# Down products with the activations held in TensorE, a rebuilt opening and new due times, in a transformer layer with 32 routed experts

## The reference, cut to what matters

```python
x = x + attn(layernorm(x), W_attn, W_proj)
x = x + ffn(layernorm(x), ...)

# attn: 16 heads of 8 channels; q against sums of k over blocks of 4, 8, ... 1024
# tokens and against the tail of the own block of 4; softmax; the same sums of v;
# out @ W_proj.T
# ffn: 32 experts of 64 hidden channels, 6 chosen for each token, 1 shared of 256
h = relu2(einsum('th,eih->tei', x, up_w)) * combine[:, :, None]
moe_out = einsum('tei,ehi->th', h, down_w)
shared = relu2(x @ shared_up_w.T) @ shared_down_w.T
return moe_out + shared
```

## Time and the profile before

| what | value |
|---|---|
| median of 3 runs | 650.69 us (650.59 to 652.74) |
| profiled execution, its own time | 650.5 us |
| its span, first to last instruction | 648.4 us |
| mean granted clock of PE | 0.930 of full speed |
| busy share of PE, DVE, ACT, POOL | 86%, 59%, 59%, 44% |

### The profile page before, as it was taken

The page is one execution under the profiler, slowest core; times in us unless marked ns, Lnnn a source line. Parts: engine busy times, 40 slices in busy tenths (PEclk is TensorE's granted clock), DMA queues, the critical chain, the costliest instruction groups (busy, mean ns, idle before and its releaser), DMA issues.

```text
span 648.4 us, 10506 instructions
## 1 busy us (share of the span) xinstructions
PE 560.4 (86%) x3568; PEld 271.1 (42%) x3568; DVE 380.3 (59%) x935; ACT 380.4 (59%) x543; POOL 282.1 (44%) x403
## 2 busy tenths in 40 slices
PE   1434778888897999889999979999998999999997
PEld 1132123243343435345445334544445434566553
DVE  2626876966878583677756991765767703605400
ACT  1310136674654686467675568677666698675764
POOL 2400303702622573335535662436436424565675
PEclk9755579898997998979999989999999999999999
DMA  6484000184320208605214049334205222234352
GB/s 154 132 210 86 1 3 3 45 208 129 83 68 25 79 4 226 178 35 129 75 50 136 31 126 211 104 85 105 75 27 162 71 67 82 85 114 144 102 175 87
DMA packets 49337, 63.45 MB, mean 98 GB/s; under 512 B 8484, under 2 KB 30788, under 8 KB 48004
## 3 DMA queue, kind: packets, MB, share of 16 engines
q1 hardware_dynamic: 49284, 62.78, 35.7%
HBM read 50.31 MB, written 12.06 MB: 96 GB/s over the span
## 4 chain that ended last, share of the span: by engine, by line
PE 58%; DVE 17%; SPq 9%; DMA 6%; issue 4%; ACT 3%; POOL 2%; POOLq 0%; DVEq 0%; ACTq 0%
PE sums_ps L1060 16%; PE ring L1048 13%; PE sums_ps L992 9%; DVE MXR L1162 6%; SPq L598 6%; PE ring L975 4%; PE ring L953 3%; DMA XP<-in_x_dram 3%; PE ring L913 2%; PE ring L970 2%; PE ring L999 2%; PE ring L1027 2%; PE ring L947 2%; DMA WB<-combine 2%; DMA QA<-MB 1%
## 5 line engine op out<-in xcount | busy, mean ns | idle before, releaser
L727 POOL TENSOR_TENSOR H<-RV,WB 128x512 f32<-128x512 f32 x128 | 164.2, 1295 | 164.5 <-ACT RV L830 130.1
L819 ACT ACTIVATE PT<-ring 128x1024 f32<-128x1024 f32 x160 | 158.5, 1022 | 96.5 <-PE ring L975 95.8
L1162 DVE TENSOR_REDUCE MXR<-ring 128x4 f32<-128x1024 f32 (+2 forms) x192 | 176.0, 952 | 61.3 <-PE ring L953 58.3
L1060 PE MATMUL sums_ps<-H,wdown 128*128 128x512 f32 x288 | 149.4, 616 | 1.4 <-POOL H L727 1.1
L877 ACT ACTIVATE RV<-ring 128x512 f32<-128x512 f32 x144 | 85.5, 594 | 74.8 <-PE ring L1048 72.8
L992 PE MATMUL sums_ps<-PT,VA 128*32 128x512 f32 (+1 forms) x768 | 91.7, 560 | 0.0
L1048 PE MATMUL ring<-XH,WUH 128*128 128x512 f32 x144 | 80.8, 561 | 2.4 <-DVE MB L1273 1.7
L830 ACT ACTIVATE RV<-RV 128x512 f32<-128x512 f32 x128 | 80.6, 630 | 3.7
L975 PE MATMUL ring<-QA,KA 54*128 54x512 bf16 (+1 forms) x384 | 61.7, 359 | 8.3 <-DMA QA<-MB 5.0
L1060 PEld LDWEIGHTS sums_ps<-H,wdown 128*128 128x128 f32 x288 | 48.8, 189 | 38.1 <-issue 25.3
L953 PE MATMUL ring<-KA,QA 51*128 51x256 bf16 (+7 forms) x512 | 61.9, 308 | 0.0
(11 more groups left out here) (128 smaller groups left out, 660.6 us busy)
## 6 DMA issues: line engine op xcount, KB each, us to landing
WB<-combine SPq DMA_DIRECT2D x256, 128.0 KB, 2.9
QA<-q_parts SPq DMA_DIRECT2D x16, 384.0 KB, 6.3
q_parts<-Qparts SPq DMA_DIRECT2D x16, 192.0 KB, 3.9
KA<-k_parts SPq DMA_DIRECT2D x8, 384.0 KB, 5.7
XP<-in_x_dram SPq DMA_DIRECT2D x4, 512.0 KB, 6.1
X<-in_x_dram SPq DMA_DIRECT2D x4, 512.0 KB, 4.9
q_parts<-Qparts SPq DMA_DIRECT2D x16, 128.0 KB, 3.6
out_dram<-OT SPq DMA_DIRECT2D x8, 256.0 KB, 2.4
```

Source lines behind the costliest of these rows:

```text
L727: pool.tensor_tensor(H[:, m % NHB, :], RV[:, m % NRV, :], WB[:, r % NWB, :], ALU.mult).then_inc(s_had, 1)
L819: act.activation(dst, src, ACT.Exp, scale=SCALE).then_inc(s_expa, 1)
L1060: pe.matmul(dsum, wdown[:, CHUNKS[n], :], H[:, m % NHB, :], start=(n == 0), stop=(n == NCH - 1)).then_inc(s_dn, 1)
L1162: ins = dve.reduce_max(MXR[:, g, i, :, q0:q0 + nq], pair("max", b, w, g, n)[:, :, at:at + ns * nq].rearrange("p e (q s) -> p e q s", s=ns) ...
```

## The change

1. `dn` holds 128 tokens of `H` and streams 128 columns of `wdown`, four times for a unit. `dsum` then has tokens on its partitions. `devac` and `yT` are gone. `fin` reads `dsum` itself and waits for the last `dn`; the first `dn` of the next window waits for `fin`.
2. ACT does an `Exp` of one element on a new tile `first` as its first work. PE does `WARM` = 30 float32 matmuls of zeros, 128x128 on 128 columns, before anything else.
3. For the first batch ACT issues half of the stores of k and q (`kst_odd`, `qst_odd`: three transfers each), and SP the other half. Later batches are as before.
4. `whigh` and `wlow` get the due time 25.0 (before -20.0). The planner's latencies of `xload`, of `KA` and `QA` loads and of `rows` are longer, and due times, `STAY` and `AHEAD` have other values, so every engine's order may be another.

```diff
-      "pe": ("fill", "max", "mT", "exp", "pv", "oT", "aT", "proj", "xT", "logits", "up", "dn", "cT", "yT"),
+ON = {"act": ("evac", "expa", "oevac", "et", "kst_odd", "qst_odd", "aTe", "xhe", "sco", "relu", "sq", "cTe", "whigh"),
+      "pe": ("fill", "max", "mT", "exp", "pv", "oT", "aT", "proj", "xT", "logits", "up", "dn", "cT"),
...
-            put(("stats1", b, h), "dve", 0.8, (("xload", b), 3.5))
+            put(("stats1", b, h), "dve", 0.8, (("xload", b), 5.0 if b else 3.5))
...
+        put(("kst", b), "sp", 3.9 if b else 2.0, ("ksplit", b, 1), later(old("kld", b - 1), 5.0))
+        if b == 0:
+            put(("kst_odd", b), "act", 2.0, ("ksplit", b, 1))
...
-            put(("devac", b, w), "act", 0.48, (("dn", b, NCH * (w + 1) - 1), 0.24), later(old("yst", b - 1, w), 2.5))
-            put(("yT", b, w), "pe", 0.44, ("devac", b, w))
-            put(("fin", b, w), "dve", 0.6, ("yT", b, w))
+            put(("fin", b, w), "dve", 0.6, ("dn", b, NCH * (w + 1) - 1), later(old("yst", b - 1, w), 2.5))
...
-SWITCH, STAY = 0.09, 4.9
-STARTUP, PERIOD = 40.0, 103.4
-OFF = {"att0": -46.6, "att1": 49.2, "ffn0": 109.3, "ffn1": 163.9, "prep": -51.0, "post": -32.9, "max": -44.2}
-UNIT_T = 3.8
-AHEAD = {"pe": 0, "act": 0.19, "dve": 0, "pool": 0.38, "sp": 0.29}
+SWITCH, STAY = 0.09, 18.4
+STARTUP, PERIOD = 40.0, 101.1
+OFF = {"att0": -38.9, "att1": 44.6, "ffn0": 96.0, "ffn1": 156.6, "prep": -20.5, "post": 5.3, "max": -48.5}
+UNIT_T = 3.1
+AHEAD = {"pe": 0, "act": 0.03, "dve": 0, "pool": 0.32, "sp": 1.72}
...
+    if kind in ("whigh", "wlow"):
+        return 25.0
...
+        def store_pieces(eng, dst, parts, pieces, signal, halves):
+
+            for a, js in enumerate(pieces):
+                for e in halves:
+                    to = dst[e, js].rearrange("j d q s -> (d q) j s")
+                    _, n, size = to.shape
+                    eng.dma_start(to, parts[HALF * e:HALF * e + HALF, a].unsqueeze(1).to_broadcast([HALF, n, size])).then_inc(signal, 16)
...
+            act.wait_ge(s_init, 2)
+            act.activation(first[:, :], zeros[:, 0:1], ACT.Exp)
...
+                elif kind == "kst_odd":
+                    act.wait_ge(s_ksplit, 1)
+                    store_pieces(act, Kd, Kparts, K_PIECES, s_kd, (1,))
...
-                pe.matmul(dsum, wdown[:, CHUNKS[n], :], H[:, m % NHB, :], start=(n == 0), stop=(n == NCH - 1)).then_inc(s_dn, 1)
-
+                for i in range(WT):
+                    ins = pe.matmul(dsum[:, P * i:P * i + P], H[:, m % NHB, P * i:P * i + P], wdown[:, CHUNKS[n], :],
+                                    start=(n == 0 and i == 0), stop=(n == NCH - 1), skip_group_check=True)
+                ins.then_inc(s_dn, 1)
+
+            pe.wait_ge(s_init, 2)
+            for _ in range(WARM):
+                pe.matmul(ring[:, 0, 0:P], zeros[:, 0:P], zeros[:, 0:P], start=True, stop=True)
...
-                    dve.wait_ge(s_yt, N("yT", b, w))
-                    dve.tensor_tensor(Y[:, w, :, :], single("yT", b, w).rearrange("p (i c) -> p i c", i=WT),
+                    dve.wait_ge(s_dn, N("dn", b, NCH * (w + 1) - 1))
+                    if b:
+                        dve.wait_ge(s_out[w], 16 * b)
+                    dve.tensor_tensor(Y[:, w, :, :], dsum.rearrange("p (i c) -> p i c", i=WT),
```

More of the change, by code:

```diff
@@ L98 @@
 PIECES = len(PART_PAIRS)
+WARM = 30
 def unit_of(r):
@@ L201, in work @@
                     back = pv_number(b, w, g, step_of_exp(w, n)) - NPT
-                    put(("exp", b, w, g, n), "pe", 0.23 + (0.11 * nh // 2 if c // 2 == w else 0), (("rows", b, w, g), 1.2),
+                    put(("exp", b, w, g, n), "pe", 0.23 + (0.11 * nh // 2 if c // 2 == w else 0), (("rows", b, w, g), 1.5),
                         ("pv", back // PVN) + PVS[back % PVN] if back >= 0 else ("wlow", 0))
@@ L243, in work @@
             put(("dn", b, u), "pe", 0.87, ("sq" if is_shared(u) else "had", b, u),
-                (("devac", b, 0) if w else ("devac", b - 1, 1)) if first else None)
+                (("fin", b, 0) if w else ("fin", b - 1, 1)) if first else None)
         for w in range(NW):
-            put(("devac", b, w), "act", 0.48, (("dn", b, NCH * (w + 1) - 1), 0.24), later(old("yst", b - 1, w), 2.5))
-            put(("yT", b, w), "pe", 0.44, ("devac", b, w))
-            put(("fin", b, w), "dve", 0.6, ("yT", b, w))
+            put(("fin", b, w), "dve", 0.6, ("dn", b, NCH * (w + 1) - 1), later(old("yst", b - 1, w), 2.5))
             put(("yst", b, w), "sp", 0.42, ("fin", b, w))
@@ L255 @@
 NBANK, SINGLES = 6, (4, 5)
-BANKS = {"max": 2, "exp": 2, "fill": 2, "up": 1, "mT": 1, "oT": 1, "aT": 1, "proj": 1, "xT": 1, "logits": 1, "cT": 1, "yT": 1}
+BANKS = {"max": 2, "exp": 2, "fill": 2, "up": 1, "mT": 1, "oT": 1, "aT": 1, "proj": 1, "xT": 1, "logits": 1, "cT": 1}
 FREED_BY = {"max": "red", "exp": "expa", "fill": "evac", "up": "relu", "mT": "mcopy", "oT": "ocopy", "aT": "aTe", "proj": "x1",
-            "xT": "xle", "logits": "sco", "cT": "cTe", "yT": "fin"}
+            "xT": "xle", "logits": "sco", "cT": "cTe"}
 ROWS_OF = {"max": 64, "exp": 64, "pv": 32}
-SWITCH, STAY = 0.09, 4.9
-STARTUP, PERIOD = 40.0, 103.4
-OFF = {"att0": -46.6, "att1": 49.2, "ffn0": 109.3, "ffn1": 163.9, "prep": -51.0, "post": -32.9, "max": -44.2}
-UNIT_T = 3.8
-AHEAD = {"pe": 0, "act": 0.19, "dve": 0, "pool": 0.38, "sp": 0.29}
-SHIFT = {"mT": -13.9, "pv": 6.3, "dn": 25.0, "had": 4.6, "red": -9.3, "fill": -5.8, "mfin": 13.6, "rows": 3.0, "ocopy": -9.6, "exp": -5.6, "oT": -4.2}
+SWITCH, STAY = 0.09, 18.4
[3 more added lines that the diff above has]
+AHEAD = {"pe": 0, "act": 0.03, "dve": 0, "pool": 0.32, "sp": 1.72}
+SHIFT = {"kld": 6.2, "relu": -9.3, "sq": 2.8, "up": -2.1, "aT": -15.2, "tails": 29.1, "split": 3.5, "evac": -40.5, "qst": 17.7, "oevac": 30.7, "max": 7.1, "mT": -17.6, "pv": 3.6, "dn": 18.5, "had": 12.9, "red": -8.6, "fill": -15.2, "mfin": 7.3, "rows": 1.3, "ocopy": 3.1, "exp": -7.5, "oT": 21.7}
 ATTEND = ("max", "red", "mfin", "split", "mT", "mcopy", "rows", "exp", "expa", "pv", "oevac", "oT", "ocopy", "td", "et", "tailw")
 FFN = ("up", "relu", "sq", "bc", "had", "dn")
-FINISH = ("devac", "yT", "fin", "yst")
+FINISH = ("fin", "yst")
 PREP = ("xload", "stats1", "aggr1", "rstd1", "apply1", "fill", "evac", "tails", "sums", "ksplit", "qsplit", "prod", "kst", "kld", "qst",
-        "qld", "xres", "whigh", "wlow")
+        "qld", "xres", "whigh", "wlow", "kst_odd", "qst_odd")
 def due(name):
@@ L426, in build @@
         zeros = sb("zeros", [P, WT * NE])
+        first = sb("first", [P, 1])
         XN = sb("XN", [P, NT, C])
@@ L618, in store_q @@
                     sp.wait_ge(s_qa[w], 32 * b)
-                store_pieces(Qd[w], Qparts[:, :, window(w)], Q_PIECES, s_qd[w])
+                store_pieces(sp, Qd[w], Qparts[:, :, window(w)], Q_PIECES, s_qd[w], (0, 1) if b else (0,))
             def load_q(b, w):
```

44 lines of the change are left out of this document (16 added, 28 removed).

## The result

| kernel | median | runs | ratio to before, 95% interval | profiled span | clock |
|---|---|---|---|---|---|
| before | 650.86 us | 4 | | 648.4 us | 0.930 |
| changed | 618.56 us | 4 | 0.9498 [0.9476, 0.9519] | 616.0 us | 0.944 |

The changed kernel is 32 us faster. Medians are over all executions of a kernel; the ratios leave out two slow ones further down, one of e13 (707.6 us, at a clock of 0.72) and one of e3 (651.2 us).

What follows compares the result with a forecast made beforehand. PE was taken to bound 390 to 590 us, one chain of engines and transfers the opening. 650.5 - 12.6 (opening) + 4.3 (`dn`) - 3.0 (`yT`) - 1.4 (end) - 4 (order) = 633.8 us; range 621 to 645.5 us.

Steps and rivals of the forecast that it cites:

- the order: Engines' replanned order: fewer changes between row counts on PE, -4 us, bounds -14 and, on the slow side, a rival.
- The second rival: PE from 110 to 390 us: the order also closes half its idle time, -12.5 us, 625.3 us; chance 0.15.
- The opening: Start up to the first `red`: 12.6 us gained from engines and transfers, bounds 3.6 and 16.9.
- The engines' 3.6 us: Opening: table load off the chain 1.28, warm transposes 0.85, warm k fill 1.51 us; k's stores at 25.5 us.
- the transfers: Opening, k's stores to first `max`: 3.87 MB at full share, 16.8 us, first `max` at 42.3 us.
- The first rival: Opening's transfers stay the bound (or clock falls, or DVE stands for x), order gives nothing: 645.1 us; chance 0.17.
- The wait for `fin` at nothing: Next window's first `dn` waiting for DVE's `fin` at 7 places: taken as nothing, bound 7 us.
- The third and fourth rivals: Third: late preparation leaves PE idle, 670 us, chance 0.07. Fourth: `dn` weight loads and streams don't overlap, +220 us, chance 0.02.

Runs made afterwards that it cites:

- e13: Changed kernel with `wlow` behind `prod` in DVE's list and, on SP, q's stores ahead of k's load: 616.7 us, ratio 0.9446.
- e3: Kernel before with only the new due times, `STAY`, `AHEAD` and latencies, replanned; old `dn` and old opening: 646.76 us, ratio 0.989.
- e7: Changed kernel with the old due times, `STAY` and `AHEAD`, replanned: 646.22 us, ratio 0.9936.
- e9: Changed kernel measured again, unchanged, as the measure for other runs: 617.52 us, ratio 0.9481.
- e2: Kernel before with the new `dn` alone, in the old order, `fin` placed by hand: 654.95 us, ratio 1.0055.
- e6: Changed kernel without its opening (no first `Exp`, no zeros, six stores on SP): 622.36 us, ratio 0.9572.
- e14: Changed kernel with 12 and 8 matmuls of zeros in front of PE's two longest waits behind the opening: 615.35 us, ratio 0.9433.
- e1: Kernel before with the new opening alone, ACT's stores put into its list by hand, order otherwise old: 647.76 us, ratio 0.9941.
- e10: Changed kernel with `wlow` put behind `prod` in DVE's list, all else the same: 618.02 us, ratio 0.9477.
- e12: Kernel before with `PERIOD` 103.5 for 103.4, replanned: 656.33 us, ratio 1.0079.
- e4: Changed kernel in its own order with the old wide matmul in `dn`, output left transposed in blocks: 614.56 us, ratio 0.9437.
- e5: Changed kernel's order with the whole old `dn` put back, `devac` and transposes (into `dsum`'s bank) included: 624.57 us, ratio 0.9595.
- e8: Changed kernel with `PERIOD` 101.2 for 101.1, so that the planner chooses anew: 630.25 us, ratio 0.9672.
- e11: Changed kernel with batch 1's statistics again ahead of the first `red` in DVE's list: 621.83 us, ratio 0.9537.
- e15: Changed kernel with the edits of e13 and e14 together and `WARM` 40 in place of 30: 613.88 us, ratio 0.9415.

## Why the prediction was right and wrong

**The failed step is the last term of the sum, the order: "I take -4, with bounds of -14 (half of the 25.1 us of idle PE too)".** With the values alone changed (e7 to e9) it is 0.9936 - 0.9481 = 4.6%, 30 us; from e2 to e6, where the latencies and the place of `fin` change too, 1.0055 - 0.9572 = 4.8%, 31 us. My -4 was the changes between row counts. Counted in PE's list they fell from 388 to 355, 33 x 0.10 = 3.3 us, so that part was sized well. Two parts were not. The windows of e2, then of e6:

```profile
90.00:290.00 200.00, 175.21 (x1431) 94.18 (x1427) 137.72 (x327) 117.69 (x154) 78.53 (x141) 0.94 0.33 87
290.00:650.00 360.00, 345.37 (x2711) 238.67 (x2710) 192.66 (x492) 242.38 (x365) 182.69 (x215) 1.00 0.34 101
```

```profile
90.00:290.00 200.00, 185.01 (x1517) 105.17 (x1515) 146.97 (x357) 126.71 (x173) 89.60 (x147) 0.96 0.38 98
290.00:622.00 332.00, 322.93 (x2595) 225.59 (x2591) 190.17 (x457) 226.52 (x342) 171.29 (x205) 0.99 0.36 103
```

PE's idle time after 90 us fell from 24.8 + 14.6 = 39.4 in e2 to 15.0 + 9.1 = 24.1 us in e6, 15.3 us, which I had only as a rival. And I had put no price on the clock, although row 0.83 of 190 to 210 us stood there: 0.94 of full speed over 200 us is 24 us at half speed (e2), 0.96 is 16 (e6), worth some 4 us of work. That makes 15.3 + 3.3 + 4 = 23 of the 28 us between the two spans, 652.3 and 624.0. The first `red` comes 4.3 us earlier in e6 (52.00, not 56.30), but this lead can't simply be added: the first projection comes no earlier (114.74 in e6, 113.93 in e2). The same account for e7 and e9 (idle time 34.4 and 22.8, changes 392 and 355, clock 0.94 and 0.98) gives 11.6 + 3.7 + 8 = 23 of 29 us. It is an account read from profiles; that an item costs its own length was tried only for the clock (e14), and some 5 us stay open. My bound was added up wrongly, too: -4 and half of 25.1 are -16.5, not -14. But what made it wrong is that it had room for half the idle time of one region and for nothing else: not for the clock, and not for what e7 and e9 leave open.

**The second rival came true as to PE's idle time.** From 110 to 390 us it went from 25.1 to 12.1 us, the half that the rival had said. Its 625.3 us, at 0.15, stood nearest to 618.6. That it came so near is in part luck: it priced the order at 12.5 us, which brought 30, and had the opening at 12.6, which brought 6.

**The opening was sized too high.** I took 12.6 us; the first `red` came 8.4 us earlier, and the time fell by 6 (e6 to e9), or by 4 in before's order (e1). Of the 8.4 us, 5.2 are the first `max` (51.48 and 46.24). The other 3.2 are DVE's not standing for x, which I had counted in; the planner's new values do that and not the opening's edits, for e6 has it too (first `red` at 52.00). The engines' 3.6 us came nearly as said in this profile: k's stores start 3.2 us earlier, with x 0.4 us late. In e9, where the zeros didn't bring the clock, they start at 28.64, only 0.5 us earlier than before. The term that failed is the transfers, "the other 3.87 MB at full share (196/0.85 = 231 GB/s) are 16.8 us": it was 4.0 MB at 199 GB/s and a share of 0.80, 20.3 us. `wlow` stayed in the chain, and SP's order put k's load ahead of q's stores; e10 shows that the first didn't decide, e13 that undoing both as it does wins nothing clear of noise. What splitting the stores brought is small. From k's first store to the first `max` it took 21.7 to 22.9 us in the five profiles with all stores on SP (before, e2, e3, e6, e12), and 20.1 to 22.5 us in the nine with the split and SP's order kept (e1, the changed kernel, e4, e5, e7, e8, e9, e11, e14), 1.0 us less on the mean. The rule that I had weighed, "Issuing engines are not separate DMA queues" of the Trainium skill's "DMA: Bandwidth & Descriptors", agrees: a second issuing engine saves only the time to start the transfers. The first rival's mechanism is thus what happened in the opening, and its forecast for the whole (645.1) was wrong only because the order gave more.

**`dn`, `yT`, `fin`.** The spacing of matmuls that the Trainium skill gives in "TensorE: Matmul & The Clock Gate", section "Back-to-back issue gap", would have made `dn` 2.5 times as dear. It was set aside for `proj`'s rows, and rightly: e4 has the new form 2.9 us dearer in all, my term 4.3. The transposes are gone, and the last add follows the last `dn` by 0.05 us and no longer by 1.4; no run prices the two by themselves. The wait for `fin` at nothing was wrong in the old order (4.4 us of PE's loads in e2) and nearly right in the one planned for it (0.8 us). The reason I gave, that the planner sees it, holds only if the planner is run again.

**The third and fourth rivals** didn't occur: preparation and post stage are due some 30 us later, and PE's idle time fell.

**Still open.** Why the new values give a good order with the new work and a poor one with the old, is not explained by any one stage that I could name. e8 and e12 say that a step of 0.1 in one value moves the time by 5 to 12 us, so it may be no more than that each set of values was chosen for its own work; no run tests that. How far the low clock costs by itself is shown in its direction (e14) and not in size.

## What to carry to other kernels

When a change also replans the order, measure the order by itself: put the old operations into the new order, and the new ones into the old (e5 and e2 told more than e3), and change the planner's values alone (e7 and e9). The idle time and the low-clock time of the bound engine, over its whole span, are what such a replanning can win; here a bound taken from one region's idle time was too small by half. An operation that is dearer by itself (`dn`, 3 us) can still be right, if it takes waits out of an order that is planned for it, as e5 against e9 suggests.

## What the runs showed of the hardware that I had not expected

**The matmuls of zeros don't always bring the clock.** In e9, the same kernel as the changed one, PE had done its 60 records by 9.98 us, paused for 1.96 us, and then took 1.85 us for the transposes, as cold as before:

```profile
1.03 8.95 PE L1072 MATMUL ring<-zeros 128*128 128x128 f32 x60 [1.03 <-POOL zeros L697]
11.94 1.85 PE L916 MATMUL ring<-ident,XP 128*128 128x128 f32 x8 [1.96 <-DVE XP L1121]
14.96 7.35 PE L921 MATMUL ring<-XNT,wqkv 128*128 128x512 f32 x12 [1.18 <-ACT XNT L792]
```

In the changed kernel's own profile a pause of 2.21 us did no harm, nor did the pauses of 0.60 to 2.25 us in eight other profiles with 30 such matmuls (e1, e4, e5, e7, e8, e10, e11, e14), where the transposes took 1.06 us. So the length of the pause alone doesn't tell. With 40 in place of 30 (e15) there was no pause, and the transposes took 1.04 us; one profile doesn't show that this makes it certain.

**A lead of the opening isn't kept to the full.** e9's first `red` was 2.5 us later than in the changed kernel's profile (49.48 and 46.99), its first projection only 0.5 us later (109.03 and 108.51). From the first exponential to the first copy of the sums the changed kernel's profile took 12.5 us at a clock of 0.64 (first row), e9 10.7 us at 0.80 (second row), with the same work:

```profile
66.70:79.20 12.50, 10.74 (x74) 2.79 (x76) 9.71 (x35) 6.00 (x8) 5.72 (x16) 0.64 0.01 2
```

```profile
69.20:79.90 10.70, 8.60 (x74) 2.37 (x74) 9.71 (x35) 5.98 (x8) 5.72 (x16) 0.80 0.01 1
```

So 1.8 of the 2.0 us that e9 regained were regained here, at a clock that differed from one execution to the next. They are near a third of the 6 us that the opening's edits are worth. Against the kernel before, the changed kernel leads by 7.7 us at the first exponential (66.73 and 74.44) and by 4.4 at the first projection (108.51 and 112.90).
